# Where the gathers of x[dst] are issued in a graph network kernel: all of them in the node pass

## What is computed

```python
m   = relu(x[src] + edge_attr)                        # layer 0
x   = layernorm(x + (1 + eps) * x + segment_sum(m, dst))
x   = layernorm(x + ten_steps_of_weighted_sums(x))    # layer 1
x   = layernorm(x + relational_two_matmul_layer(x))   # layer 2
e   = (x[dst] - x[src]) @ theta.T + (x @ phi.T)[src]  # layer 3
x   = layernorm(x + segment_max(e, dst))
```

## Time and profile before

| what | us |
|---|---|
| median of three runs | 4209.33 |
| span of the profiled execution (the page gives no other time of it) | 5230.0 |
| setup | 0 to 49 |
| counting stage | 49 to 417 |
| of it, zeros being written | 62 to 230 |
| node pass | 417 to 918 |
| edge pass begins | 918 |
| gathers of `xdst`: 128 in the counting stage | 50 to 219 |
| gathers of `xdst`: 272 in the node pass | 418 to 836 |

### The profile page before, as it was taken

The page is one execution under the profiler, slowest core; times in us unless marked ns, Lnnn a source line. Parts: engine busy times, 40 slices in busy tenths (PEclk is TensorE's granted clock), DMA queues, the critical chain, the costliest instruction groups (busy, mean ns, idle before and its releaser), DMA issues. The chain is left out here.

```text
span 5230.0 us, 57991 instructions
## 1 busy us (share of the span) xinstructions
PE 2653.0 (51%) x9282; PEld 1302.4 (25%) x9282; DVE 2825.2 (54%) x7308; ACT 1341.5 (26%) x4703; POOL 2738.0 (52%) x2688
## 2 busy tenths in 40 slices
PE   1270000566666665357543577767666103975543
PEld 0150000232222233112111234433333001332222
DVE  3298998566666454356432366656665223652322
ACT  0003333344333232112111233333332011431111
POOL 4406773554454455544365355555556555646565
PEclk7695555777777777678776688877887556995555
DMA  7705777555555442334422544444443243321111
GB/s 249 295 0 164 217 216 198 140 146 144 140 142 134 141 115 78 86 99 114 93 55 52 123 116 113 110 102 106 101 102 77 64 125 91 73 63 31 30 30 22
DMA packets 513328, 587.96 MB, mean 112 GB/s; under 512 B 222598, under 2 KB 402382, under 8 KB 508182
## 3 DMA queue, kind: packets, MB, share of 16 engines
q1 hardware_dynamic: 365050, 417.75, 26.1%
q0 software_dynamic: 92160, 94.65, 11.9%
q10 hardware_dynamic: 55972, 74.03, 4.4%
HBM read 289.08 MB, written 303.60 MB: 113 GB/s over the span
## 5 line engine op out<-in xcount | busy, mean ns | idle before, releaser
L508 POOL DMA_INDIRECT xdst<-in_x,dstc x400 | 447.1, 1118 | 385.0 <-PEq L667 198.6
L284 POOL DMA_INDIRECT gb<-nodes,ib x400 | 386.1, 965 | 460.4 <-ACT ib L873 338.5
L268 PE MATMUL bank<-ident,act 128*99 128x128 f32 x400 | 87.4, 357 | 642.5 <-issue 570.5
L278 PE MATMUL bank<-ident,scan 99*128 99x99 f32 (+2 forms) x1120 | 205.6, 313 | 376.8 <-DVE scan L1032 139.8
L1314 PE MATMUL bank<-e_bxT,w 105*128 105x512 f32 x432 | 252.9, 702 | 224.7 <-ACT e_hm L1233 173.1
L304 PE MATMUL bank<-chosen,rec 128*6 128x512 bf16 x1200 | 360.8, 464 | 1.1 <-ACT packed L901 0.8
L1265 POOL DMA_INDIRECT out<-e_xob,e_ob x288 | 295.5, 1026 | 101.3 <-issue 86.8
L278 PEld LDWEIGHTS bank<-ident,scan 99*128 99x128 f32 (+2 forms) x1120 | 159.3, 213 | 560.5 <-issue 559.8
L284 POOL DMA_INDIRECT ugb<-nodes,ib x160 | 170.0, 1062 | 240.5 <-ACT ib L1984 158.5
L586 PE MATMUL bank<-hot_at,hot_no 128*125 128x400 f16 x800 | 167.9, 357 | 235.1 <-DVE hot_at L612 138.0
L284 POOL DMA_INDIRECT parent<-upper_rows,ib x160 | 159.3, 996 | 197.1 <-ACT ib L1544 148.2
(11 more groups left out here) (332 smaller groups left out, 7175.9 us busy)
## 6 DMA issues: line engine op xcount, KB each, us to landing
nodes<-wt SPq DMA_DIRECT2D x40, 1286.2 KB
lone_rows<-gb ACTq DMA_DIRECT2D x100, 294.0 KB
e_lsb<-lone_rows SPq DMA_DIRECT2D x72, 294.0 KB
parents<-zeros SPq DMA_DIRECT2D x21, 960.0 KB
upper_rows<-tb SPq DMA_DIRECT2D x100, 194.0 KB
deep_sum<-zeros SPq DMA_DIRECT2D x20, 960.0 KB
layer<-zeros SPq DMA_DIRECT2D x20, 960.0 KB
kb<-edge_keep SPq DMA_DIRECT2D x100, 192.0 KB
```

What stands on the lines that cost most here:

```text
L268: last = nc.tensor.transpose(slot(dst_ps[0:w, :], t), rows_sb[:, t, c0:c0 + w], ident[:, :])
L278: last = nc.tensor.transpose(dst_ps[:, t, 0:w], slot(cols_sb[0:w, :], t), ident[0:w, 0:w])
L284: yield nc.gpsimd.indirect_dma_start(out=dst[s][:, t, 0:width], out_offset=None, in_=table, in_offset=bass.IndirectOffsetOnAxis(ap=ib[s][: ...
L508: nc.gpsimd.indirect_dma_start(out=xdst[:, k * F:(k + 1) * F], out_offset=None, in_=a["x"], in_offset=bass.IndirectOffsetOnAxis(ap=dstc[:, ...
```

## The change

All 100 groups are now fetched in the node pass. The counting stage's list for GpSimd is gone, and with it the constant EARLY. Lines behind the removed ones move up by 1 (behind line 31) and by 6 (behind line 561).

```diff
-EARLY = 32
...
-                @block.gpsimd
-                def _(pool):
-                    for g in range(EARLY):
-                        fetch_dst(g, s_late)
-
...
                 @block.gpsimd
                 def _(pool):
-                    for g in range(EARLY, NG):
+                    for g in range(NG):
                         fetch_dst(g, s_late)
                     pool.wait_ge(s_late, NG * 16 * T)
```

## The result

The kernel after takes 4316.53 us (median of 4 runs, 4307.42 to 4323.02), the kernel before 4206.69 us in the runs beside it: +109.8 us. The ratio is 1.0267, with a 95% interval of 1.0254 to 1.028; it is not that of the two medians, which is 1.0261. The kernel after is slower, as forecast, and its time is inside the range.

The account below looks back on a forecast made before the run. VectorE was taken to bound the node pass, with neither GpSimd nor DMA setting it. +99.5 us for added gathers and -4 us for removed ones gave +95.5 us on 4209.3, so 4305 us, range 4258 to 4340 us.

Parts of the forecast that it names:

- The bound and the cover: VectorE sets the node pass; 128 gathers leave a stage where GpSimd had 199 us spare for one with 83.
- window of 318.3 intervals: Node pass: VectorE's 489.8 us hold 318.3 gather intervals of 1.539 us, leaving 80.7 of 399 uncovered.
- Part 1: Node pass: 128 gathers added, those not covered by VectorE running at 1.25 us each, delay the edge pass by 99.5 us.
- Part 2: Counting stage: 128 gathers removed, freeing DMA time so zeros end earlier; -4 us, taken between nothing and 8.8 us.
- late groups: Counting stage: groups taking some 20 instead of 1.96 us while zeros are written; waits before line 609 total 151.6 us.
- Microseconds, not a share: The sum of +95.5 us was carried from profile to runs unscaled, being made of instruction durations and not of waits.
- (a): Node pass: gathers run at 1.25 us beside VectorE too, longer ones being a profiling effect; 4213 us, no change; chance 0.06.
- (b): Counting stage: gathers make groups wait before line 609; up to 151.6 us come back, -52 us, 4157 us; chance 0.05.
- (c): Moved gathers start before the node pass, during the counting stage; time 4209 us less at most 4; chance 0.02.
- VectorE's idle stretch: Sign in the profile after: VectorE idle some 100 us between the last line 775 and the edge pass.
- The counting stage ends within 9 us: Sign in the profile after: the counting stage should end within 9 us of where it did.
- a sign of being wrong: The forecast would be wrong if the counting stage shrank by some 100 us or more.

Follow-up runs that it names:

- Experiments 2, 3 and 5: The kernel before with EARLY = 16, 24 and 8, in that order, instead of 32: 4234.34, 4200.82 and 4271.21 us.
- Experiment 4: The kernel after, with the small inputs of VectorE's five large two-input instructions in the node pass put in PSUM: 4234.93 us, 1.0071 of the kernel before.
- experiment 1: The kernel before, unchanged, run once more for a second profile: 4210.49 us in its one run; the profile spans 4208.7 us.

## Why the prediction was right, point by point

**The bound and the cover: right.** VectorE ended the node pass, and 128 gathers did not fit into what was left of it. Experiments 2, 3 and 5 put the threshold between 304 and 336 gathers; the forecast's window of 318.3 intervals is 319 gathers, and 315 or 316 start before VectorE's end where the window is full.

**Part 1: right in kind, 99.5 us forecast and 111.7 us measured.** Two terms were small. The uncovered gathers were put at 100.9 us; they took 109.0, because 314 or so fit instead of 319 (1.55 instead of 1.539 us each) and one pause of 3.3 us fell among them. The pace of 1.539 holds two pauses of GpSimd's issue, 9.1 and 3.2 us; in the second profile the same two are 9.2 and 8.7 us, which is the whole difference between 1.54 and 1.56. The end of the stage was priced by a store, 8.8 us from the last gather's start; behind a gather it is 875.43 - 861.73 = 13.7 us, of which 6.2 pass until the landing has been counted and 5.0 go into a drain, an instruction that stands on GpSimd at the block's end. Behind VectorE's last instruction it stayed 767.22 - 756.88 = 10.3 us. So 109.0 + 13.7 - 10.3 = 112.4 us, which the trace's 111.7 confirms.

**Part 2: -4 us forecast, -3.5 us measured, for another reason; that the sizes agree is luck.** The term was built on zeros that end earlier and on late groups. The zeros do end earlier, at 215.8 instead of 229.8 us, but nothing waits for them, and the second profile has no late groups; the doubt that the text put beside them was justified. Of the 3.5 us, 1.2 were there before the stage's first instruction (49.65 against 48.48 us). For the rest there is a cause in the rows: a group beside gathers can take 2.01 us (152.17 to 154.18) where in the kernel after it takes 1.95 (149.44 to 151.39). In the second profile 39 of the 87 groups that start beside gathers take 2.01 or 2.02 us, which makes 39 x 0.06 = 2.3 us; with EARLY = 24, 16 and 8 there are 29, 19 and 8 such groups beside gathers, and in the kernel after none.

**Microseconds, not a share: right.** As a share of 5230.0 us the +95.5 us would have been 1.8% of 4209.3, 77 us. The work that the sum is made of has the same durations in both profiles of the kernel before: from the first gather of the node pass to VectorE's end it is 489.8 and 489.2 us, and VectorE is busy for 2825.2 and 2823.7 us of the whole.

**The rivals.** (a), gathers at 1.25 us beside VectorE and long ones only by profiling: fallen. The second profile, with gathers as long, cannot decide this, being a profile too, though it shows that the 1021 us do not come with profiling; the runs' times decide it, as 368 gathers cost 64 us with the hold and nothing without it. Experiment 4 shows what the rival would have given, +32 us, more than the 7.5 worked out: of the difference, 19 us are three pauses of 4 to 8 us in GpSimd's issue, and 5 the longer end of the stage. (b), late groups that come back: fallen with experiment 1; there was nothing to win. (c), gathers that start early: fallen, GpSimd waited 260.25 us for the counting stage to end, without a list of its own there.

**The signs named.** VectorE's idle stretch was put at some 100 us and is 122.67; GpSimd's at a few us and is 13.70. "The counting stage ends within 9 us" is met against the second profile (3.5 us) and missed by 145 us against the first. Against the first, from which it was read, even a sign of being wrong came true: the counting stage is 154 us shorter there, more than the 100 named. A sign read from a profile that far from the runs could not be trusted in either direction, and the 1021 us should have been a reason to say so there.

## What to carry to other kernels

Work that is off the path is not free to move: count it against the slack of the stage into which it goes, at the pace it has there beside that stage's other engines, and price what sticks out at its own pace. Where indirect transfers from GpSimd run beside VectorE, look at which VectorE instructions read two operands from SBUF; putting the small operand into PSUM gave back 78 of 110 us here, but only because GpSimd had become the bound. And hold the span of a profile against the timed runs before reading waits from it.

## What the runs showed of the hardware that was not expected

- A gather that starts under a VectorE instruction with two large SBUF operands ends 0.80 to 0.88 us after it (193 gathers of the kernel after); with one operand in PSUM, none of the 400 took over 1.2 us, at unchanged VectorE durations (1.16 us). Moving the small operand is enough: `nm` is 20 numbers a partition, read as 960.
- Behind a gather the end of a block costs more than behind a store, and not a fixed amount: 13.7 us from the last gather's start here and in experiment 4, 17.7 with EARLY = 16 and 11.1 with 8, against 10.3 us from VectorE's last instruction. The trace's records of GpSimd's sequencer show a drain there after the landing has been counted, of 5.0, 5.0, 9.0 and 2.4 us, and of 3.8 and 6.4 us with EARLY = 32 and 24. That is 0.082 to 0.083 us for each gather issued since the last pause of GpSimd's issue (61, 61, 110, 29, 46 and 78 gathers), and in every trace such a pause, of 3.2 to 9.4 us, comes after each 113 gathers of a stage. What the drain waits for is open.
- In the first profile TensorE's reports to VectorE came late while the DMA engines were at 0.99: products that had ended at 64.65 us were reported at 83.47 us, and the next, ended at 71.73, at 104.51. In the second profile, with the same gathers and zeros and the DMA engines at 0.99 again, they did not, nor with EARLY = 24 and 16. The cause was not found.
